# Attention scores of a float32 block: one float32 matmul per head in place of a product split into high and low parts

## The chip, the cores and the metric

The kernel runs on one core of one Trainium2 chip. The metric is the device time of one execution in microseconds (us), as the median of the runs; lower is better.

## The reference, cut to what matters

Eight sequences of 128 tokens with 512 features go through a layer norm, a cross-attention with 32 query heads and 8 key/value heads of 128 features, a gated residual, a second layer norm and a gated feed-forward layer. All of it is float32.

```python
q = (query @ Wq).reshape(nb, q_len, H, D).transpose(0, 2, 1, 3)
k = (key @ Wk).reshape(nb, q_len, KVH, D).transpose(0, 2, 1, 3)
...
q = q * cos + _rotate_half(q) * sin
k = k * cos + _rotate_half(k) * sin
...
scores = jnp.einsum('bhqd,bhkd->bhqk', q, k) / jnp.sqrt(jnp.float32(D))
scores = jnp.where(mask == 0, jnp.float32(-1000000000.0), scores)
attn = jax.nn.softmax(scores, axis=-1)
```

The mask holds a 1 where a position is masked out of the context and 0 elsewhere, one mask per sequence.

## The kernel before

TensorE multiplies in the reduced type float32r. To keep float32 accuracy each float32 operand is split: ScalarE (ACT) writes a rounded high part, GpSimd (POOL) or VectorE (DVE) writes the remainder as a low part, and TensorE (PE) adds three products: high by high, high by low, low by high. The helper `three` (L509 to L511) does this for the projections, the product with v, the output projection and the feed-forward layer.

Each engine runs an order of work written out by hand, held together by semaphores. A prologue (to about 115 us) transposes context and x, makes k and v for all heads, and stores both to scratch memory in HBM. Then come 64 attention steps, numbered n: a step is one sequence and one group of four query heads that share a key/value head. `pair(gg, c)` handles two steps, k = 0 and 1. In a pair PE makes two blocks of new queries (`q_block`, 12 matmuls of 512 columns each), scores, the transpose of the probabilities, the product with v (`pv`) and the output projection of an earlier pair. The feed-forward layer follows from about 584 us.

What the change touches, step by step:

- Rotation of queries and keys: DVE multiplies by cosine and sine (`rot_cos`, `rot_sin`), POOL adds the two (`add_q`, `add_k`) and so writes `q32` and `k32` in float32.
- Keys: `k_hi_copy` (ACT) and `k_lo_split` (POOL) write the high and low part side by side into `ks_parts`; SP's queue stores both to scratch (`store_k`) and later loads them into `k_parts` (`load_k`).
- Queries: `q_hi_copy` (ACT, L843) and `q_lo_split` (POOL, L1143) make `q_hi` and `q_lo` for each step.
- Scores (L632, L633): for each of four heads one matmul with q_hi over 256 columns (key high and low parts, side by side) and one with q_lo over 128 columns (key high part) that is added to the first half. The four heads fill two banks of PSUM, so a step's scores wait until the mask step of the step before has read them (`dve_mask >= n`).
- Mask and maximum: `mask_first` (DVE, L1432) adds the mask to the second half of the scores and writes `prob`; `mask_rest` (DVE, L1441, four custom instructions) adds the first half and takes the row minimum (the scores are negated). ACT's exponentials (L913) follow, then the reciprocal on DVE (L1451), then POOL's normalisation (`norm`, L1185), then PE's transposes (L515), which are float32 matmuls in transpose mode with an identity.

Of the kernel before, what the change touches and what calls it, by code (L numbers as in the profile page):

```python
# [76 lines left out]
def build(nc, x, ctx, pos, mask, g_x, g_f, Wq, Wk, Wv, Wo, w12, b12, w3, b3, out):  # L77
    table = nc.inline_tensor(rope_table(), "rope_table")
    table = table.ap() if hasattr(table, "ap") else table
    k_dram = nc.dram_tensor("k_scratch", [UNITS * 128, HB * 2 * S], F32, kind="Internal").ap()  # L80
# [16 lines left out]
    with es:  # L97
# [9 lines left out]
        q_hi, q_lo = place("q_hi", [128, 2, GH, S], F32R), place("q_lo", [128, 2, GH, S], F32R)  # L107
        k_parts = place("k_parts", [128, 2, HB, 2 * S], F32R)
# [26 lines left out]
        wk_hi = place("wk_hi", [128, 2, KT * 128], F32R, at["q_hi"])  # L135
        wk_lo = place("wk_lo", [128, 2, KT * 128], F32R, at["q_lo"])
        ks_parts = place("ks_parts", [128, 2, HB, 2 * S], F32R, at["o_hi"])
# [26 lines left out]
        s_parts = s_banks[:, :].rearrange("p (h two k) -> p h two k", h=GH, two=2)  # L164
# [24 lines left out]
        act_khi, pool_klo = sems("act_khi", "pool_klo")  # L189
        pe_v, act_vhi, dve_vlo = sems("pe_v", "act_vhi", "dve_vlo")  # L190
        act_qhi, pool_qlo = sems("act_qhi", "pool_qlo")
        pe_score, dve_masked, dve_mask = sems("pe_score", "dve_masked", "dve_mask")
# [164 lines left out]
        def _(sp):  # L357
# [25 lines left out]
            def store_k(kk):  # L383
                group, half = K_ORDER[kk]
                u = 2 * group + half
                sp.wait_ge(act_khi, kk + 1)
                sp.wait_ge(pool_klo, kk + 1)
                sp.dma_start(k_dram[u * 128:(u + 1) * 128, :], f32(ks_parts[:, kk % 2].rearrange("p b k -> p (b k)"))).then_inc(k_stored[kk % 2], 16)
# [12 lines left out]
            def load_k(half, group):  # L401
                sp.dma_start(f32(k_parts[:, half].rearrange("p b k -> p (b k)")),
                             k_dram[bass.ds(group * 256 + half * 128, 128), :]).then_inc(k_loaded[half], 16)
# [68 lines left out]
            def ffn_load(t):  # L472

                dst, s, _ = ffn_raw(t)
                if t < RAW:
                    sp.wait_ge(act_whi, CHUNKS - RAW + t + 1)
                    sp.wait_ge(pool_wlo, pool_split(CHUNKS - RAW + t))
                elif t == RAW:

                    sp.wait_ge(act_qhi, 4 * (UNITS - 1))  # L480
                    sp.wait_ge(pool_qlo, 4 * (UNITS - 1))
                for i in range(4):
                    sp.dma_start(dst[32 * i:32 * i + 32, :].rearrange("b (j f) -> b j f", j=4), ffn_src(t, i)).then_inc(s, 16)
# [14 lines left out]
            sp.wait_ge(pool_klo, UNITS)  # L498
# [8 lines left out]
        def _(pe):  # L507
# [114 lines left out]
            def scores(gg, c, k):  # L622
                n = n_of(gg, c, k)
                half, b = (c // 2) % 2, 2 * (c % 2) + k
                pe.wait_ge(act_qhi, n + 1)
                pe.wait_ge(pool_qlo, n + 1)
                if k == 0:
                    pe.wait_ge(k_loaded[half], 16 * (2 * gg + c // 4 + 1))
                if not (isinstance(n, int) and n < 1):
                    pe.wait_ge(dve_mask, n)  # L630
                for h in range(GH):
                    nc.tensor.matmul(s_banks[:, 256 * h:256 * (h + 1)], q_hi[:, k, h, :], k_parts[:, half, b, :], start=True, stop=False)  # L632
                    mm = nc.tensor.matmul(s_banks[:, 256 * h:256 * h + 128], q_lo[:, k, h, :], k_parts[:, half, b, 0:128], start=False, stop=True)  # L633
                mm.then_inc(pe_score, 1)
# [204 lines left out]
        def _(act):  # L839
# [54 lines left out]
            def q_hi_copy(gg, c, k):  # L894

                n = n_of(gg, c, k)
                b = 2 * (c % 2) + k
                if isinstance(n, int) and n < 2:
                    act.wait_ge(pool_rope, ROT_ORDER.index(("Q", 3)) + 1)
                else:  # L900
                    act.wait_ge(pool_rope, KBLOCKS + 16 * gg + 4 * (c // 2) + 4)
                if isinstance(n, int) and n < 2:

                    act.wait_ge(pe_kq, ROT_ORDER.index(("K", 6 + n, 1)) + 1)
                else:
                    act.wait_ge(pe_score, n - 1)
                hi(q_hi[:, k], q32[:, (c // 2) % 2, :, b * S:(b + 1) * S], act_qhi)

# [15 lines left out]
            def o_hi_copy(gg, c, k):  # L924
                n = n_of(gg, c, k)
                act.wait_ge(pe_pv, n + 1)
                if isinstance(n, int) and n < 2:

                    act.wait_ge(k_stored[0], 16 * KBLOCKS // 2)
                    act.wait_ge(k_stored[1], 16 * KBLOCKS // 2)  # L930
                else:
                    act.wait_ge(pe_out, n - 1)
                hi(o_hi[:, k], k4(pv_bank[:, :]), act_ohi)
# [8 lines left out]
            kk = vi = 0  # L942
            for i, blk in enumerate(STAGE):
# [5 lines left out]
                if i == 34:  # L949
                    q_hi_copy(0, 0, 0)  # L950
                if i == 35:
                    q_hi_copy(0, 0, 1)
                if i == 36:
                    exps(0, 0, 0)
                if i in (2, 3) or i > 3 and STAGE[i - 1][0] == "K":
                    k_hi_copy(kk)
                    kk += 1
# [13 lines left out]
            def first_pair():  # L971
# [3 lines left out]
                q_hi_copy(0, 1, 0)  # L975
                exps(0, 0, 1)
                q_hi_copy(0, 1, 1)
# [6 lines left out]
            def pair(gg, c):  # L984
# [6 lines left out]
                q_hi_copy(gg, c + 1, 0)  # L991
                o_hi_copy(gg, c, 0)
                pT_hi_copy(gg, c, 1)
                q_hi_copy(gg, c + 1, 1)
# [42 lines left out]
            q_hi_copy(3, 3, 0)  # L1037
# [4 lines left out]
            q_hi_copy(3, 3, 1)  # L1042
# [4 lines left out]
            q_hi_copy(3, 4, 0)  # L1047
# [3 lines left out]
            q_hi_copy(3, 4, 1)  # L1051
# [3 lines left out]
            q_hi_copy(3, 5, 0)  # L1055
            o_hi_copy(3, 3, 0)
            q_hi_copy(3, 5, 1)
# [8 lines left out]
            q_hi_copy(3, 6, 0)  # L1066
# [3 lines left out]
            q_hi_copy(3, 6, 1)  # L1070
            pT_hi_copy(3, 5, 0)
            o_hi_copy(3, 4, 1)
            q_hi_copy(3, 7, 0)
# [4 lines left out]
            q_hi_copy(3, 7, 1)  # L1078
# [52 lines left out]
        def _(pool):  # L1131
# [22 lines left out]
            def add_k(r, kk):  # L1154
                pool.wait_ge(dve_rot, r + 1)
                if kk >= 2:
                    pool.wait_ge(act_khi, kk - 1)
                    pool.wait_ge(pool_klo, kk - 1)
                nc.gpsimd.tensor_tensor(k32[:, kk % 2], t_cos[:, r % 2, :], t_sin[:, r % 2, :], ALU.add).then_inc(pool_rope, 1)

            def k_lo_split(kk):
                pool.wait_ge(act_khi, kk + 1)
                minus(ks_parts[:, kk % 2, :, S:2 * S], k4(k32[:, kk % 2]), f32(ks_parts[:, kk % 2, :, 0:S]), pool_klo)

            def add_q(gg, e, r=None):
# [6 lines left out]
                else:  # L1172

                    pool.wait_ge(act_qhi, 16 * gg + 4 * (e // 4) - 4)
                    pool.wait_ge(pool_qlo, 16 * gg + 4 * (e // 4) - 4)
                nc.gpsimd.tensor_tensor(q32[:, (e // 4) % 2, e % 4, :], t_cos[:, ts, :], t_sin[:, ts, :], ALU.add).then_inc(pool_rope, 1)  # L1176

            def q_lo_split(gg, c, k):
                b = 2 * (c % 2) + k
                pool.wait_ge(act_qhi, n_of(gg, c, k) + 1)  # L1180
                minus(q_lo[:, k], q32[:, (c // 2) % 2, :, b * S:(b + 1) * S], f32(q_hi[:, k]), pool_qlo)
# [12 lines left out]
            for i, blk in enumerate(STAGE):  # L1194
                if i == 34:
                    q_lo_split(0, 0, 0)
                if i == 36:
                    q_lo_split(0, 0, 1)
                    norm(0, 0, 0)
                if i and STAGE[i - 1][0] == "K":  # L1200
                    k_lo_split(kk)
                    kk += 1
                if blk[0] == "K":
                    add_k(r, kk)
                    r += 1
# [7 lines left out]
            def first_pair():  # L1213
                chunks = pair_chunks(0, 0)
                q_lo_split(0, 1, 0)
# [3 lines left out]
                q_lo_split(0, 1, 1)  # L1219
# [5 lines left out]
            def pair(gg, c):  # L1225
# [7 lines left out]
                q_lo_split(gg, c + 1, 0)  # L1233
                q_lo_split(gg, c + 1, 1)
# [15 lines left out]
            q_lo_split(3, 3, 0)  # L1250
# [4 lines left out]
            q_lo_split(3, 3, 1)  # L1255
# [4 lines left out]
            q_lo_split(3, 4, 0)  # L1260
            q_lo_split(3, 4, 1)
# [3 lines left out]
            q_lo_split(3, 5, 0)  # L1265
            add_q(3, 12)
            q_lo_split(3, 5, 1)
# [6 lines left out]
            q_lo_split(3, 6, 0)  # L1274
            q_lo_split(3, 6, 1)
# [4 lines left out]
            q_lo_split(3, 7, 0)  # L1280
            norm(3, 6, 1)
            q_lo_split(3, 7, 1)
# [12 lines left out]
        def _(dve):  # L1295
# [127 lines left out]
            def mask_first(gg, c, k):  # L1423

                n = n_of(gg, c, k)
                dve.wait_ge(pe_score, n + 1)
                if not (isinstance(n, int) and n < 2):
                    dve.wait_ge(pe_pT, n - 1)
                b = (2 * c + k) % B
# [5 lines left out]
            def mask_rest(gg, c, k):  # L1435

                n = n_of(gg, c, k)
                dve.wait_ge(dve_masked, n + 1)
# [6 lines left out]
            def mask_scores(gg, c, k):  # L1445
                mask_first(gg, c, k)
                mask_rest(gg, c, k)
# [39 lines left out]
            def pair(gg, c):  # L1487
# [4 lines left out]
                mask_first(gg, c, 1)  # L1492
                recip(gg, c, 0)
                mask_rest(gg, c, 1)
# [235 lines left out]
```

## Time and profile before

| | |
|---|---|
| median of 3 runs | 665.45 us (664.97 to 665.58) |
| span of the profiled execution, first to last instruction | 662.9 us |
| PE busy | 654.6 us (99% of the span), granted clock 1.000 |
| DVE, ACT, POOL busy | 490.2, 314.1, 385.5 us |
| DMA | 66.32 MB moved |

The profile gives the span of its execution and no separate device time for it; the median of the runs is 2.55 us above that span. Matmul records overlap: one begins while the one before still drains, so the time that a matmul occupies the engine is read from the distance between starts, not from its duration.

### The profile page before, as it was taken

To read this page: it belongs to the slowest core of one execution; us is meant where nothing else is said; L and a number is where in the kernel's file an instruction comes from. 1 tells how busy PE (TensorE), PEld (TensorE's weight loads), DVE (VectorE), ACT (ScalarE), POOL (GpSimd) and SP (SyncE) were. 2 spreads that over 40 slices of the span, in tenths; PEclk is the share of its full clock that TensorE was granted. 3 is DMA by queue.
4 is the path that set the end of the run, shared out by engine and by line. 5 is a ranking of instruction groups with operands and counts; after the bars stand their busy time and mean duration, and the time that the engine had idled before them with its cause. 6 is when DMAs were issued, how large, how long until landed. Compare 5 with 4: busy or idle time off the path is not lost.

```text
span 662.9 us, 11265 instructions
## 1 busy us (share of the span) xinstructions
PE 654.6 (99%) x3309; PEld 550.3 (83%) x3309; DVE 490.2 (74%) x1235; ACT 314.1 (47%) x891; POOL 385.5 (58%) x323
## 2 busy tenths in 40 slices
PE   8999999999999999999999999999999999989998
PEld 7888888788888888888888888888888888878886
DVE  3987665887777777777777777777777888986432
ACT  4335613545445445544554554554455566545210
POOL 6457767875566666666556666666655776402100
PEclk9999999999999999999999999999999999999999
DMA  9996983422212131312222121212122205000002
GB/s 302 321 325 210 306 303 105 143 62 99 91 39 97 44 99 34 95 32 96 62 80 95 34 98 45 95 32 95 63 76 75 58 10 151 0 1 1 0 33 95
DMA packets 67452, 66.32 MB, mean 100 GB/s; under 512 B 6608, under 2 KB 50640, under 8 KB 67408
## 3 DMA queue, kind: packets, MB, share of 16 engines
q1 hardware_dynamic: 65984, 64.77, 30.7%
q0 software_dynamic: 384, 1.05, 0.4%
q8 instruction: 17, 0.28, 0.2%
q14 instruction: 27, 0.22, 0.1%
q10 hardware_dynamic: 1040, 0.00, 0.1%
HBM read 46.93 MB, written 18.87 MB: 99 GB/s over the span
## 4 chain that ended last, share of the span: by engine, by line
PE 94%; DVE 2%; DMA 1%; issue 1%; POOL 0%; ACT 0%; DVEq 0%
PE f_bank L509 12%; PE f_bank L511 12%; PE f_bank L510 12%; PE o_bank L509 10%; PE o_bank L511 10%; PE o_bank L510 10%; PE s_banks L632 6%; PE t_bank L515 4%; PE pv_bank L509 3%; PE pv_bank L511 3%; PE pv_bank L510 3%; PE s_banks L633 2%; PE t_bank L511 1%; PE t_bank L509 1%; PE s_banks L511 1%; PE s_banks L510 1%
## 5 line engine op out<-in xcount | busy, mean ns | idle before, releaser
L1185 POOL TENSOR_TENSOR prob<-prob,small 128x512 f32<-128x512 f32 x64 | 66.6, 1040 | 124.9 <-DVE small L1451 124.9
L913 ACT ACTIVATE prob<-prob,small 128x128 f32<-128x128 f32 x256 | 99.8, 391 | 77.7 <-DVE small L1441 72.2
L509 PE MATMUL o_bank<-wo_hi,o_hi 128*128 128x512 f32 x248 | 102.1, 412 | 0.0
L1143 POOL TENSOR_TENSOR q_lo<-q,q_hi 128x512 fp32r<-128x512 f32 x64 | 82.7, 1292 | 32.8 <-ACT q_hi L843 32.8
L509 PE MATMUL f_bank<-xT_hi,wq_hi 128*128 128x512 f32 x256 | 101.6, 397 | 0.0
L843 ACT ACTIVATE o_hi<-pv_bank 128x512 fp32r<-128x512 f32 x64 | 38.3, 599 | 131.4 <-PE pv_bank L511 130.9
L511 PE MATMUL f_bank<-xT_hi,wq_lo 128*128 128x512 f32 x256 | 99.9, 390 | 0.0
L510 PE MATMUL f_bank<-xT_lo,wq_hi 128*128 128x512 f32 x256 | 99.8, 390 | 0.0
L511 PE MATMUL o_bank<-wo_hi,o_lo 128*128 128x512 f32 x248 | 97.4, 393 | 0.0
L510 PE MATMUL o_bank<-wo_lo,o_hi 128*128 128x512 f32 x248 | 96.9, 391 | 0.0
L1353 DVE TENSOR_TENSOR t_sin<-f_bank,rope 64x512 f32<-64x512 f32 x128 | 88.1, 689 | 2.8
L1176 POOL TENSOR_TENSOR q<-t_cos,t_sin 128x512 f32<-128x512 f32 x64 | 82.7, 1293 | 4.3 <-DVE t_sin L1353 4.2
L1441 DVE CUSTOM_DVE_ANT_0 prob<-s_banks,prob 128x128 f32<-128x128 f32 x256 | 59.1, 287 | 10.3 <-DVE prob L1432 7.7
L1353 DVE TENSOR_TENSOR t_cos<-f_bank,rope 128x512 f32<-128x512 f32 x64 | 43.9, 686 | 29.5 <-PE f_bank L511 29.4
L632 PE MATMUL s_banks<-k_parts,q_hi 128*128 128x256 f32 x256 | 62.8, 323 | 0.4 <-issue 0.2
L1465 DVE SCALAR_TENSOR_TENSOR resid<-o_bank,small,resid 128x512 f32<-128x512 f32 x62 | 46.4, 748 | 17.4 <-PE o_bank L511 16.2
L633 PE MATMUL s_banks<-k_parts,q_lo 128*128 128x128 f32 x256 | 56.9, 222 | 0.0
L511 PEld LDWEIGHTS f_bank<-xT_hi,wq_lo 128*128 128x128 f32 x256 | 48.1, 188 | 10.2
L509 PEld LDWEIGHTS f_bank<-xT_hi,wq_hi 128*128 128x128 f32 x256 | 48.1, 188 | 9.5 <-issue 0.4
L510 PEld LDWEIGHTS f_bank<-xT_lo,wq_hi 128*128 128x128 f32 x256 | 48.2, 188 | 9.1
L511 PEld LDWEIGHTS o_bank<-wo_hi,o_lo 128*128 128x128 f32 x248 | 46.6, 188 | 10.6
L1306 DVE TENSOR_TENSOR o_lo<-pv_bank,o_hi 128x512 fp32r<-128x512 f32 x64 | 44.0, 687 | 15.3 <-ACT o_hi L843 15.3
(170 smaller groups left out, 1469.5 us busy)
## 6 DMA issues: line engine op xcount, KB each, us to landing
k_scratch<-ks_parts SPq DMA_DIRECT2D x16, 512.0 KB, 3.1
raw<-in_L_xattn_Wq_dram SPq DMA_DIRECT2D x32, 256.0 KB, 2.8
raw<-in_L_xattn_Wo_dram SPq DMA_DIRECT2D x32, 256.0 KB, 2.6
k_parts<-k_scratch SPq DMA_DIRECT2D x16, 512.0 KB, 3.6
v_scratch<-vs_hi SPq DMA_DIRECT2D x16, 256.0 KB, 3.9
v_scratch<-vs_lo SPq DMA_DIRECT2D x16, 256.0 KB, 4.3
v_hi<-v_scratch SPq DMA_DIRECT2D x16, 256.0 KB, 3.9
v_lo<-v_scratch SPq DMA_DIRECT2D x16, 256.0 KB, 4.3
```

The costliest lines, as they stand in the source:

```text
L509: nc.tensor.matmul(dst, st[0], mv_[0], start=start, stop=False)
L510: nc.tensor.matmul(dst, st[0], mv_[1], start=False, stop=False)
L511: return nc.tensor.matmul(dst, st[1], mv_[0], start=False, stop=stop)
L632: nc.tensor.matmul(s_banks[:, 256 * h:256 * (h + 1)], q_hi[:, k, h, :], k_parts[:, half, b, :], start=True, stop=False)
L633: mm = nc.tensor.matmul(s_banks[:, 256 * h:256 * h + 128], q_lo[:, k, h, :], k_parts[:, half, b, 0:128], start=False, stop=True)
L913: e = nc.scalar.activation(prob[:, k, h, :], prob[:, k, h, :], ACT.Exp, bias=nmin[k][:, h:h + 1], scale=-1.0, accum_out=psum_row[k][:, h:h ...
L1143: nc.gpsimd.tensor_tensor(dst, a, b_, ALU.subtract).then_inc(s, 1)
L1176: nc.gpsimd.tensor_tensor(q32[:, (e // 4) % 2, e % 4, :], t_cos[:, ts, :], t_sin[:, ts, :], ALU.add).then_inc(pool_rope, 1)
L1185: nc.gpsimd.tensor_tensor(prob[:, k], prob[:, k], rrow[k].unsqueeze(2).to_broadcast([128, GH, S]), ALU.mult).then_inc(pool_norm, 1)
L1353: return nc.vector.tensor_tensor(dst, a, b_, ALU.mult)
L1441: op = nc.vector.tensor_tensor_reduce(prob[:, k, h, :], s_parts[:, h, 0, :], prob[:, k, h, :], 1.0, HUGE, ALU.add, ALU.min, nmin[k][:, h:h ...
L1465: nc.vector.scalar_tensor_tensor(out=resid[:, b, :], in0=bank_of_out(gg, c, k)[:, :], scalar=tg_x, in1=resid[:, b, :], op0=ALU.mult, op1=A ...
```

## The change

The scores become one float32 matmul per head of 128 columns, stationary `q32`, moving `k_ring` (the keys in float32). The split parts of q and k go, with the ACT and POOL instructions that make them; the scratch for k and the ring that it is loaded into are half as large. Each step's scores take one PSUM bank, and steps use the two banks in turn, so scores of step n wait for the mask of step n - 2 only. The mask is an operand of the four custom instructions; `mask_first` goes. Some waits change their source: the store of k waits for POOL's add, `add_k` waits for the store two blocks back to have landed, `add_q` waits for scores in place of the copies, scores wait for POOL's add, and the load of the last feed-forward weights waits for scores. The buffers `wk_hi` and `wk_lo` get space of their own.

```diff
-            def k_hi_copy(kk):
-                act.wait_ge(pool_rope, ROT_ORDER.index(("K",) + K_ORDER[kk]) + 1)
-                if kk >= 2:
-                    act.wait_ge(k_stored[kk % 2], 16 * (kk // 2))
-                hi(ks_parts[:, kk % 2, :, 0:S], k4(k32[:, kk % 2]), act_khi)
...
-                hi(q_hi[:, k], q32[:, (c // 2) % 2, :, b * S:(b + 1) * S], act_qhi)
...
-            def k_lo_split(kk):
-                pool.wait_ge(act_khi, kk + 1)
-                minus(ks_parts[:, kk % 2, :, S:2 * S], k4(k32[:, kk % 2]), f32(ks_parts[:, kk % 2, :, 0:S]), pool_klo)
...
-            def q_lo_split(gg, c, k):
-                b = 2 * (c % 2) + k
-                pool.wait_ge(act_qhi, n_of(gg, c, k) + 1)
-                minus(q_lo[:, k], q32[:, (c // 2) % 2, :, b * S:(b + 1) * S], f32(q_hi[:, k]), pool_qlo)
...
             def scores(gg, c, k):
                 n = n_of(gg, c, k)
                 half, b = (c // 2) % 2, 2 * (c % 2) + k
-                pe.wait_ge(act_qhi, n + 1)
-                pe.wait_ge(pool_qlo, n + 1)
                 if k == 0:
+                    if isinstance(n, int) and n == 0:
+                        pe.wait_ge(pool_rope, ROT_ORDER.index(("Q", 3)) + 1)
+                    else:
+                        pe.wait_ge(pool_rope, KBLOCKS + 16 * gg + 4 * (c // 2) + 4)
                     pe.wait_ge(k_loaded[half], 16 * (2 * gg + c // 4 + 1))
-                if not (isinstance(n, int) and n < 1):
-                    pe.wait_ge(dve_mask, n)
+                if not (isinstance(n, int) and n < 2):
+                    pe.wait_ge(dve_mask, n - 1)
                 for h in range(GH):
-                    nc.tensor.matmul(s_banks[:, 256 * h:256 * (h + 1)], q_hi[:, k, h, :], k_parts[:, half, b, :], start=True, stop=False)
-                    mm = nc.tensor.matmul(s_banks[:, 256 * h:256 * h + 128], q_lo[:, k, h, :], k_parts[:, half, b, 0:128], start=False, stop=True)
+                    mm = nc.tensor.matmul(s_bank[k][:, 128 * h:128 * (h + 1)], q32[:, (c // 2) % 2, h, b * S:(b + 1) * S], k_ring[:, half, b, :],
+                                          start=True, stop=True)
                 mm.then_inc(pe_score, 1)
...
             def add_k(r, kk):
                 pool.wait_ge(dve_rot, r + 1)
                 if kk >= 2:
-                    pool.wait_ge(act_khi, kk - 1)
-                    pool.wait_ge(pool_klo, kk - 1)
+                    pool.wait_ge(k_stored[kk % 2], 16 * (kk // 2))
...
-                nc.vector.tensor_tensor(prob[:, k], s_parts[:, :, 1, :], mfill[:, b, :].unsqueeze(1).to_broadcast([128, GH, S]),
-                                        ALU.add).then_inc(dve_masked, 1)
...
                 for h in range(GH):
-                    op = nc.vector.tensor_tensor_reduce(prob[:, k, h, :], s_parts[:, h, 0, :], prob[:, k, h, :], 1.0, HUGE,
+                    op = nc.vector.tensor_tensor_reduce(prob[:, k, h, :], s_bank[k][:, 128 * h:128 * (h + 1)], mfill[:, b, :], 1.0, HUGE,
                                                         ALU.add, ALU.min, nmin[k][:, h:h + 1])
```

## Rows read from the trace of the kernel before

**Rows 1.** The page: busy us, share of the span, instructions of each engine.

```profile
PE 654.6 (99%) x3309; PEld 550.3 (83%) x3309; DVE 490.2 (74%) x1235; ACT 314.1 (47%) x891; POOL 385.5 (58%) x323
```

**Rows 2.** The chain that ended last: shares of the span by engine.

```profile
PE 94%; DVE 2%; DMA 1%; issue 1%; POOL 0%; ACT 0%; DVEq 0%
```

**Rows 3.** Stretches: window, then busy us (count) of PE, PEld, DVE, ACT, POOL; clock.

```profile
300.00:400.00 100.00, 99.86 (x517) 84.30 (x516) 76.22 (x210) 50.20 (x164) 62.88 (x53) 1.00 0.25 78
```

**Rows 4.** Waits of PE: total us, times, longest us.

```profile
PE s_banks L515 <- ACT xnorm L1009: 1.9, 1, 1.9
...
PE s_banks L632 <- DVE small L1441: 0.2, 1, 0.2
```

**Rows 5.** Timeline of PE around one step's scores: start us, duration us, instruction.

```profile
301.36 0.28 PE L632 MATMUL s_banks<-k_parts,q_hi 128*128 128x256 f32 x1
301.47 0.22 PE L633 MATMUL s_banks<-k_parts,q_lo 128*128 128x128 f32 x1
...
302.23 0.45 PE L509 MATMUL f_bank<-xT_hi,wq_hi 128*128 128x512 f32 x1
302.51 0.40 PE L510 MATMUL f_bank<-xT_lo,wq_hi 128*128 128x512 f32 x1
302.75 0.39 PE L511 MATMUL f_bank<-xT_hi,wq_lo 128*128 128x512 f32 x1
...
304.79 0.39 PE L511 MATMUL f_bank<-xT_hi,wq_lo 128*128 128x512 f32 x1
305.02 0.60 PE L515 MATMUL t_bank<-ident,prob 128*128 128x128 f32 x4
305.37 0.48 PE L509 MATMUL o_bank<-wo_hi,o_hi 128*128 128x512 f32 x1
305.69 0.39 PE L510 MATMUL o_bank<-wo_lo,o_hi 128*128 128x512 f32 x1
```

**Rows 6.** Timeline of PE's weight loads for the same scores.

```profile
301.36 0.19 PEld L633 LDWEIGHTS s_banks<-k_parts,q_lo 128*128 128x128 f32 x1
...
302.05 0.19 PEld L633 LDWEIGHTS s_banks<-k_parts,q_lo 128*128 128x128 f32 x1
```

**Rows 7.** PE's groups by shape: busy us, mean ns of one.

```profile
L633 PE MATMUL s_banks<-k_parts,q_lo 128*128 128x128 f32 x256 | 56.9, 222 | 0.0
L515 PE MATMUL t_bank<-ident,prob 128*128 128x128 f32 x256 | 38.5, 272 | 0.2
```

**Rows 8.** Groups that the change removes, and the custom instruction beside them.

```profile
L1143 POOL TENSOR_TENSOR q_lo<-q,q_hi 128x512 fp32r<-128x512 f32 x64 | 82.7, 1292 | 32.8 <-ACT q_hi L843 32.8
L1143 POOL TENSOR_TENSOR ks_parts<-k,ks_parts 128x512 fp32r<-128x512 f32 x16 | 20.8, 1299 | 12.6 <-ACT ks_parts L843 12.6
L843 ACT ACTIVATE q_hi<-q 128x512 fp32r<-128x512 f32 x64 | 40.1, 626 | 9.6 <-POOL q L1176 8.3 <-PE f_bank L511 1.4
L843 ACT ACTIVATE ks_parts<-k 128x512 fp32r<-128x512 f32 x16 | 10.1, 633 | 25.8 <-POOL k L1159 25.8
L1432 DVE TENSOR_TENSOR prob<-s_banks,mfill 128x512 f32<-128x512 f32 x64 | 44.2, 691 | 6.5 <-PE s_banks L633 5.3 <-PE t_bank L515 0.7
```

**Rows 9.** Timeline of DVE, ACT and PE at the end of attention.

```profile
571.41 0.69 DVE L1432 TENSOR_TENSOR prob<-s_banks,mfill 128x512 f32<-128x512 f32 x1 [0.23 <-PE t_bank L515]
...
575.22 0.60 ACT L843 ACTIVATE pT_hi<-t_bank 128x512 fp32r<-128x512 f32 x1 [0.30 <-PE t_bank L515]
...
576.01 0.68 DVE L1306 TENSOR_TENSOR pT_lo<-t_bank,pT_hi 128x512 fp32r<-128x512 f32 x1
...
584.34 0.66 PE L515 MATMUL s_banks<-ident,xnorm 128*128 128x128 f32 x4 [1.86 <-ACT xnorm L1009]
```

**Rows 10.** DMA issues: count, KB each, median us from issue to landing.

```profile
k_scratch<-ks_parts SPq DMA_DIRECT2D x16, 512.0 KB, 3.1
...
k_parts<-k_scratch SPq DMA_DIRECT2D x16, 512.0 KB, 3.6
```

**Rows 11.** Waits of SP's queue: total us, times, longest us.

```profile
SPq L387 <- POOL ks_parts L1143: 54.2, 16, 10.6
```

More of the change, by code:

```diff
@@ L106, in build @@
         q32 = place("q32", [128, 2, GH, HT], F32)
-        q_hi, q_lo = place("q_hi", [128, 2, GH, S], F32R), place("q_lo", [128, 2, GH, S], F32R)
-        k_parts = place("k_parts", [128, 2, HB, 2 * S], F32R)
+        wk_hi, wk_lo = place("wk_hi", [128, 2, KT * 128], F32R), place("wk_lo", [128, 2, KT * 128], F32R)
+        k_ring = place("k_ring", [128, 2, HB, S], F32)
         v_hi, v_lo = place("v_hi", [128, 2, HB, D], F32R), place("v_lo", [128, 2, HB, D], F32R)
@@ L134, in build @@
         w3_all = place("w3_all", [128, KT, E], F32, at["wq_lo"])
-        wk_hi = place("wk_hi", [128, 2, KT * 128], F32R, at["q_hi"])
-        wk_lo = place("wk_lo", [128, 2, KT * 128], F32R, at["q_lo"])
-        ks_parts = place("ks_parts", [128, 2, HB, 2 * S], F32R, at["o_hi"])
         ffn_raw2 = place("ffn_raw2", [128, 4, 512], F32, at["q32"])
@@ L163, in build @@
         o_bank = [bank("o_bank0"), bank("o_bank1")]
-        s_parts = s_banks[:, :].rearrange("p (h two k) -> p h two k", h=GH, two=2)
+        s_bank = [s_banks[:, 0:512], s_banks[:, 512:1024]]
         up_bank = [f_bank[0][:, :], f_bank[1][:, :], s_banks[:, 0:512], s_banks[:, 512:1024]]
@@ L385, in store_k @@
                 u = 2 * group + half
-                sp.wait_ge(act_khi, kk + 1)
-                sp.wait_ge(pool_klo, kk + 1)
-                sp.dma_start(k_dram[u * 128:(u + 1) * 128, :], f32(ks_parts[:, kk % 2].rearrange("p b k -> p (b k)"))).then_inc(k_stored[kk % 2], 16)
+                sp.wait_ge(pool_rope, ROT_ORDER.index(("K", group, half)) + 1)
+                sp.dma_start(k_dram[u * 128:(u + 1) * 128, :], k32[:, kk % 2]).then_inc(k_stored[kk % 2], 16)
             v_rows = v_dram.rearrange("(h g t p) c -> h g t p c", h=2, g=KVH, t=2)
@@ L892, in x_norms @@
                     normalise(xnorm[:, b % 4, :], b)
-            def q_hi_copy(gg, c, k):
-                n = n_of(gg, c, k)
-                b = 2 * (c % 2) + k
[L898 to L906, printed above, removed]
-                hi(q_hi[:, k], q32[:, (c // 2) % 2, :, b * S:(b + 1) * S], act_qhi)
             def exps(gg, c, k):
@@ L926, in o_hi_copy @@
                 act.wait_ge(pe_pv, n + 1)
[L927 to L931, printed above, removed]
+                if not (isinstance(n, int) and n < 2):
                     act.wait_ge(pe_out, n - 1)
@@ L941, in _ @@
                 first_chunk(s)
-            kk = vi = 0
+            vi = 0
             for i, blk in enumerate(STAGE):
@@ L1194, in _ @@
             for i, blk in enumerate(STAGE):
-                if i == 34:
-                    q_lo_split(0, 0, 0)
                 if i == 36:
-                    q_lo_split(0, 0, 1)
                     norm(0, 0, 0)
-                if i and STAGE[i - 1][0] == "K":
-                    k_lo_split(kk)
-                    kk += 1
                 if blk[0] == "K":
                     add_k(r, kk)
+                    kk += 1
                     r += 1
@@ L1421, in _, with mask_scores @@
                     nc.vector.tensor_scalar(mfill[:, :, :], mask_raw[:, :, :], 0.0, MASKED, ALU.is_equal, ALU.mult).then_inc(dve_small, 1)
-            def mask_first(gg, c, k):
+            def mask_scores(gg, c, k):
                 n = n_of(gg, c, k)
+                b = (2 * c + k) % B
                 dve.wait_ge(pe_score, n + 1)
```

61 lines of the change are left out of this document (6 added, 55 removed).

## The prediction

> **What bounds the kernel now.** I read the busy times first, then the chain that ended last, then PE's waits, and only then single stretches. PE is busy for 654.6 of 662.9 us, no other engine for more than 74% [rows 1], and 94% of the chain is PE itself [rows 2]. In a stretch of steady attention PE is busy for 99.86 of 100 us at a granted clock of 1.00, the 2.4 GHz level, while DVE has 24, POOL 37 and ACT 50 us to spare [rows 3]. PE is idle for 8.3 us in all; its largest wait is 1.9 us for the second layer norm, and for the mask step it waits 0.2 us, once [rows 4]. So the reader is to see one thing: work taken from DVE, ACT or POOL is worth nothing by itself. The change is worth what it does to PE's own instructions, and a little at the waits.
>
> **What a step's scores cost PE today.** Starts count, not durations. Matmuls of 512 columns follow each other at (304.79 - 302.75) / 9 = 0.227 us [rows 5], 0.057 us for each 128 columns. The scores begin at 301.36; the projection after them begins at 302.23 and its second matmul at 302.51 [rows 5]. That first projection matmul takes 0.28 and not 0.227, because its weights could not be loaded ahead in time. So the scores displace 302.51 - 301.36 - 0.227 = 0.923 us. The columns explain less: 4 heads of 384 columns are 4 x 0.170 = 0.68 us. The loads explain it: eight, at (302.05 - 301.36) / 6 = 0.115 us each [rows 6], make 0.92 us. Scores today are bound by their weight loads. 64 steps cost 59 us.
>
> **What the float32 matmul costs: the open term.** Before has no float32 matmul outside transpose mode. Its bounds come from these rows.
>
> - Below: the transposes are float32, 128x128 against 128x128. Four of them displace 305.69 - 305.02 - 0.227 = 0.443 us, 0.111 us each [rows 5], about twice the 0.057 us of 128 float32r columns. The durations agree: 272 ns against 222 ns for 128 columns [rows 7], 50 ns more for an equal shape. If a head costs no more than one transpose, a step falls from 0.923 to 0.443, 0.48 less; 64 of them are 31 us.
> - Above: a float32 product written as four products of high and low parts, each with its own load at today's 0.115 us, is 0.46 a head and 1.84 a step: 0.917 x 64 = 59 us more.
> - Between: in a transpose one operand is an identity, so only the other needs its full width. Here both need it, which doubles the pass: 2 x 0.111 = 0.222 a head, 0.887 a step. Counted the other way: today's split streams three products, 384 columns; a full product adds low by low, 512 columns, 0.227 a head and 0.907 a step if two loads of 0.115 hide under it, which they just do.
>
> I take the middle of these two, 0.897 a step: the row for a float32 pass and the row for 512 columns agree within 2%, while the ends differ by a factor of four. That is 0.026 less than 0.923, times 64, 1.7 us less. Steps ahead of `pv` are bound by the same eight loads, so I give them the same price.
>
> The Trainium skill speaks against this middle at one place. TensorE: Matmul & The Clock Gate, section Terms, says that transpose mode makes a float32 matmul four times faster. By that rule a head would cost 4 x 0.111 = 0.444 us, as an estimate, and the sum would be 54 us more in place of 1.7 less; no run here shows a float32 matmul without that mode.
>
> **The wait between steps.** The scores of step n wait today for the mask of step n - 1, because all four heads fill both banks; afterwards for n - 2. That 0.2 us [rows 4] is the gain. The new waits on `pool_rope` replace waits on instructions that themselves waited for it, and the query blocks are ready a pair earlier, so nothing new is late there. `add_q` now waits for scores instead of copies before it overwrites `q32`. Queued behind it on POOL are chunk splits and normalisations, which PE needs. But the sine product that `add_q` also needs stands behind the mask of those very scores in DVE's order, so the new wait has always ended: nothing.
>
> **Work removed off the path.** DVE loses 64 x 691 ns = 44 us, ACT 64 x 626 + 16 x 633 ns = 50 us, POOL 64 x 1292 + 16 x 1299 ns = 103 us [rows 8]. PE hides all of it today; were PE not there, DVE would still be the fullest. The mask as an operand of the custom instructions changes one input from `prob` to `mfill`, both float32 in SBUF, so I leave their price alone.
>
> One place has no cover: the end of attention, where PE idles 1.86 us for the layer norm behind a row of DVE work [rows 9]. The mask add at 571.41 stands in that row and costs 0.69 plus about 0.2 until the next instruction. But later in the row DVE takes pT_lo at 576.01, and that needs ACT's pT_hi, which ends at 575.82. DVE cannot move ahead of it by more than 0.19, so of 0.9 us about 0.15 arrives; what is late next is PE's transpose.
>
> **Keys.** Stores and loads halve from 512 KB [rows 10]. The prologue is PE's, so this buys nothing. `add_k` now waits for a store to land, with SP's queue ahead of it; behind it on POOL stand weight splits that PE needs. A store lands 3.1 us after issue, and SP has waited 54.2 us in total for POOL's key split [rows 11], so SP is early rather than late. Store and reuse lie two key blocks apart, in most of the prologue with two value blocks of 12 matmuls between them, 4 x 12 x 0.227 = 11 us. Nothing; uncovered, each late store would cost PE up to its 3 us.
>
> **Sum.** 1.7 + 0.2 + 0.15 = 2.05 us off a span of 662.9: 660.85. The median of the runs is 665.45, 2.55 us above the span; I carry that over and predict 663.4 us.
>
> **Rivals.**
>
> 1. Loads stay the bound. If a float32 head still needs two loads and each takes its 0.115 plus a few ns as today, a step is 0.92 to 0.95 us. For: loads bind today [rows 6]. Against: the transposes run at 0.111 with loads in their stream [rows 5]. Between 0 and +1.7 us on PE, less 0.35 at the waits: 665 to 666.5, no change that can be told.
> 2. Loads are not hidden at all. After a short pass the next load shows as 0.05 us today (0.28 against 0.227) [rows 5]. If each head pays that, 0.05 x 4 x 64 = 13 us come on top: 676 us. It decides once more than 0.02 us a head is exposed (0.02 x 256 = 5 us).
> 3. Four full passes, the other side at its plainest: 0.444 to 0.46 a head, so 1.77 to 1.84 a step, 54 to 59 us more on an engine that has no room to hide it: 719 to 724 us. For: four products are what two full-width operands hold, and today's split leaves one out to save time. Against: the 0.111 of a transpose is already twice a float32r pass, so four times that would count the width twice. It decides as soon as a head takes more than 0.231 us, today's price. The skill's rule on transpose mode, above, is this rival.
> 4. One pass, as cheap as a transpose: 665.45 - 31 = 634 us. For: same type and shape [rows 7]. Against: the row carries an identity.
>
> **How the numbers follow.** Forecast 0.43, with its own range of 661.5 to 664.1; rival 1 0.16; rival 2 0.13; rival 3 0.22; rival 4 0.06. A measurement of this kernel tells about 0.2% (1.3 us) from no change. The forecast and rival 4 are faster: 0.49. Rival 1 is the same, 0.14 of it within the bound and 0.02 beyond. Rivals 2 and 3 are slower: 0.37 with that. Leaving out rival 3 would leave more than 2 in 10 outside, so the range reaches over it: 661 to 722. Only rival 4 and the edges lie outside.
>
> **What would show it.** In the profile after, the distance from the first score matmul to the second matmul behind the scores, less 0.227, is the step's price: 0.89 right, 0.92 rival 1, 1.1 rival 2, 1.8 rival 3, 0.44 rival 4. The number of load and matmul records per head tells the passes. q_lo, q_hi and L1432 must be gone from POOL, ACT and DVE, with the span unmoved by it. PE's wait on the mask at 0.2 us must be gone, and the wait before the layer norm's transposes should stay near 1.7 us. Wrong would be a wait of POOL on the key store, or PE waiting for `pool_rope`.

## The result, and the profile after

| | before | after |
|---|---|---|
| median, us (4 runs each) | 665.21 (664.97 to 665.58) | 660.7 (660.45 to 661.0) |
| ratio of the medians | | 0.9932, 95% interval 0.9918 to 0.9946 |
| span of the profiled execution, us | 662.9 | 659.0 |

The change made the kernel faster by 4.5 us; 663.4 was predicted, and 660.7 lies just under the low edge, 661. The direction and the price of the float32 matmul came out as forecast. The gain at the waits was several times the forecast, and the price of the scores before was read too low.

The page of the profile after, busy time and chain, answers to [rows 1] and [rows 2]:

```profile
PE 651.8 (99%) x3309; PEld 549.5 (83%) x3309; DVE 448.1 (68%) x1171; ACT 271.4 (41%) x811; POOL 285.8 (43%) x243
...
PE 96%; DMA 1%; DVE 1%; POOL 0%; issue 0%; ACT 0%
```

DVE lost 42 us, ACT 43 and POOL 100, about what [rows 8] promised, and PE 2.8. PE's count of 3309 is the same as before: 512 pairs of load and matmul for the scores then, 512 now. The groups of the scores' line say so, with mean ns of one at the end:

```profile
L626 PE MATMUL s_banks<-k_ring,q 128*128 128x128 f32 x512 | 67.3, 274 | 0.0
...
L626 PEld LDWEIGHTS s_banks<-k_ring,q 128*128 128x128 f32 x512 | 66.7, 191 | 4.7
```

There are 256 heads in 64 steps, so one float32 matmul of the program is two loads and two matmuls on the engine. Each lasts 274 ns, beside 272 for a transpose [rows 7]. The stretch in steady attention and PE's waits, as in [rows 3] and [rows 4]:

```profile
300.00:400.00 100.00, 100.00 (x517) 84.41 (x517) 69.29 (x199) 42.96 (x144) 48.51 (x41) 1.00 0.19 58
```

```profile
PE s_banks L507 <- ACT xnorm L967: 1.7, 1, 1.7
PE pv_bank L583 <- POOL ident L1082: 1.5, 1, 1.5
PE pv_bank L501 <- issue: 0.6, 1, 0.6
```

The wait for the mask is gone, no wait on `pool_rope` has come, and the layer norm's has gone from 1.86 to 1.69 us. The timeline of PE around a step, as in [rows 5]:

```profile
298.95 1.05 PE L626 MATMUL s_banks<-k_ring,q 128*128 128x128 f32 x8
299.76 0.48 PE L501 MATMUL f_bank<-xT_hi,wq_hi 128*128 128x512 f32 x1
300.07 0.40 PE L502 MATMUL f_bank<-xT_lo,wq_hi 128*128 128x512 f32 x1
```

The step's price is 300.07 - 298.95 - 0.227 = 0.893 us; 0.897 was forecast. Starts are printed to 0.01 us, so a price read from two of them can be off by as much. By the starts in ns that the trace holds, the 52 steps between 137 and 531 us cost 0.930 us each in before (0.928 to 0.931) and 0.895 in after (0.894 to 0.895).

**Where the 3.9 us of span came from.** PE's matmuls outside the scores are the same in both traces and in the same order, so I subtracted start from start. The difference grows in stages (after minus before, worked out from the two timelines of PE):

| stretch of before, us | gained, us | predicted, us |
|---|---|---|
| start, up to 43 us (first loads) | 0.14 | 0 |
| first four score steps, 114 to 137 | 1.22 | some 0.3 (0.2 for the mask wait, 4 x 0.026) |
| 52 steps, 137 to 531, without the next row | 1.84 | 1.4 (52 x 0.026) |
| two turns of the loop over pairs, at 260 and 381 | 0.25 + 0.34 | 0 |
| last eight steps, 531 to 580 | -0.13 | 0.2 |
| layer norm, from 580 | 0.21 | 0.15 |

The start is no effect of the change: profiles of the variants below differ there by up to 0.47 us, and it is taken off their differences.

**The first score step.** Here is the trace of before on POOL, on PE's weight loads and on PE, at the first scores:

```profile
113.34 1.29 POOL L1143 TENSOR_TENSOR q_lo<-q,q_hi 128x512 fp32r<-128x512 f32 x1 [0.74 <-ACT q_hi L843]
...
114.70 0.19 PEld L632 LDWEIGHTS s_banks<-k_parts,q_hi 128*128 128x128 f32 x1 [0.59 <-issue]
...
114.14 0.39 PE L511 MATMUL f_bank<-cT_hi,wk_lo 128*128 128x512 f32 x1
114.73 0.36 PE L632 MATMUL s_banks<-k_parts,q_hi 128*128 128x256 f32 x1 [0.20 <-issue]
```

and PE of after at the same place:

```profile
114.01 0.39 PE L503 MATMUL f_bank<-cT_hi,wk_lo 128*128 128x512 f32 x1
114.23 1.05 PE L626 MATMUL s_banks<-k_ring,q 128*128 128x128 f32 x8
```

POOL's q_lo ends at 114.63, the load follows at 114.70; without q_lo the scores follow the matmul ahead by 0.22 us, not 0.59. The releaser is given as "issue", with 0.20 on PE because the last matmul's record still drains, and with 0.59 on the weight loads. A reader who goes by PE's waits alone sees a third of it.

**The turns of the loop.** Here are ACT's wait row, its timeline at 256 us and the instruction queue's row (packets, MB, share) of the trace of before:

```profile
ACT prob L913 <- issue: 5.3, 2, 2.7
...
256.49 0.40 ACT L913 ACTIVATE prob<-prob,small 128x128 f32<-128x128 f32 x1 [2.61 <-issue]
...
q14 instruction: 27, 0.22, 0.1%
```

In after, ACT has no such row, and the queue moves fewer packets:

```profile
q14 instruction: 16, 0.13, 0.1%
```

ACT stands still for 2.6 us at each of two turns, by the profile without another engine to wait for, and PE's transposes come late by 0.25 and 0.34 us.

### The profile page after: what moved, and what is told of

Read it like the earlier page. It is cut to its first block, busy times and chain, and to the rows that moved or that the text cites. A ratio compares the mean times of both kernels' runs of the same rounds, so it can differ in the third digit from the quotient of the medians.

```text
span 659.0 us, 10792 instructions
## 1 busy us (share of the span) xinstructions
PE 651.8 (99%) x3309; PEld 549.5 (83%) x3309; DVE 448.1 (68%) x1171; ACT 271.4 (41%) x811; POOL 285.8 (43%) x243
## 4 chain that ended last, share of the span: by engine, by line
PE 96%; DMA 1%; DVE 1%; POOL 0%; issue 0%; ACT 0%
PE f_bank L503 12%; PE f_bank L501 12%; PE f_bank L502 12%; PE o_bank L501 10%; PE o_bank L503 10%; PE o_bank L502 10%; PE s_banks L626 9%; PE t_bank L507 4%; PE pv_bank L501 3%; PE pv_bank L503 3%; PE pv_bank L502 3%; PE t_bank L501 1%; PE t_bank L503 1%; PE s_banks L503 1%; PE s_banks L501 1%; PE s_banks L502 1%
## 5 line engine op out<-in xcount | busy, mean ns | idle before, releaser
L1352 DVE CUSTOM_DVE_ANT_0 prob<-s_banks,mfill 128x128 f32<-128x128 f32 x256 | 59.2, 287 | 20.5 <-PE s_banks L626 14.3
L626 PEld LDWEIGHTS s_banks<-k_ring,q 128*128 128x128 f32 x512 | 66.7, 191 | 4.7
L626 PE MATMUL s_banks<-k_ring,q 128*128 128x128 f32 x512 | 67.3, 274 | 0.0
L1224 DVE TENSOR_TENSOR pT_lo<-t_bank,pT_hi 128x512 fp32r<-128x512 f32 x64 | 43.9, 686 | 23.6 <-ACT pT_hi L837 23.5
L1091 POOL TENSOR_TENSOR wq_lo<-raw,wq_hi 128x512 fp32r<-128x512 f32 x35 | 45.0, 1290 | 29.8 <-ACT wq_hi L837 29.8
L1091 POOL TENSOR_TENSOR wo_lo<-raw,wo_hi 128x512 fp32r<-128x512 f32 x32 | 41.2, 1292 | 35.8 <-ACT wo_hi L837 35.8
```

Source lines behind the costliest of these rows:

```text
L626: mm = nc.tensor.matmul(s_bank[k][:, 128 * h:128 * (h + 1)], q32[:, (c // 2) % 2, h, b * S:(b + 1) * S], k_ring[:, half, b, :], start=True ...
L1091: nc.gpsimd.tensor_tensor(dst, a, b_, ALU.subtract).then_inc(s, 1)
L1224: nc.vector.tensor_tensor(dst, src, f32(hi_part), ALU.subtract).then_inc(s, 1)
L1352: op = nc.vector.tensor_tensor_reduce(prob[:, k, h, :], s_bank[k][:, 128 * h:128 * (h + 1)], mfill[:, b, :], 1.0, HUGE, ALU.add, ALU.min, ...
```

## The experiments

Theory after the result: the matmul gives 1.8 us over the steps, and the rest comes from waits of the first steps and at the turns, each ended by another part of the change. Rival: everything comes from the matmul, through a shorter step that moves the waits as well. Edits are against the kernel after, unless said otherwise.

**Parts put back, one at a time.** First the copies of q: q_hi and q_lo are made again, and the scores wait for both but read q32.

```diff
             def scores(gg, c, k):
+                pe.wait_ge(act_qhi, n + 1)
+                pe.wait_ge(pool_qlo, n + 1)
...
+                q_hi_copy(gg, c + 1, 0)
...
+                q_lo_split(gg, c + 1, 0)
```

> The changed kernel with q_hi (ACT) and q_lo (POOL) made again for every step, read by nobody, and the scores waiting for them as before. Theory of parts: the first step of attention waits again for POOL's q_lo (0.5 us), and ACT's loop, 16 instructions longer per turn, stands still for 2.6 us at its two turns again, of which 0.25 to 0.35 us each reach PE: 1.0 to 1.2 us more than the changed kernel, about 661.8. Rival (freed ACT and POOL speed PE up all along): 2 us more or above, spread evenly over the 64 steps.

661.29 us, ratio to before 0.9945 [0.9933, 0.9958], span 659.6. PE is later by 0.44 us at the first score step and by nothing more in the steps behind it. The weight loads' wait is back, this row of the waits of PE's loads:

```profile
PEld s_banks L630 <- issue: 0.6, 1, 0.6
```

The standstill of ACT, which I expected back as well, isn't. So the first step's wait hung on the copies, the standstill on something else.

Then the wait between steps:

```diff
-                if not (isinstance(n, int) and n < 2):
-                    pe.wait_ge(dve_mask, n - 1)
+                if not (isinstance(n, int) and n < 1):
+                    pe.wait_ge(dve_mask, n)
```

> The changed kernel with one number changed: the scores of step n wait for the mask of step n - 1 instead of n - 2, as if there were one bank. Theory of parts: only the first steps feel it, 0 to 0.4 us more, near 661.0. Rival (a bank per batch is what brings the gain): 1.5 us more or above.

661.14 us, 0.9942 [0.9929, 0.9955], span 659.3. Nothing in the first four steps; about 0.1 us at one place of each of the loop's three rounds (138, 258 and 378 us), 0.29 in all.

Then the mask add, as an instruction of its own on DVE, whose result the custom instructions overwrite:

```diff
+                nc.vector.tensor_tensor(prob[:, k], s_bank[k].rearrange("p (h k) -> p h k", h=GH), mfill[:, b, :].unsqueeze(1).to_broadcast([128, GH, S]),
+                                        ALU.add).then_inc(dve_masked, 1)
```

> The changed kernel with the mask add of 691 ns put back on DVE ahead of the four custom instructions, in the order of the kernel before; its output is written over. Theory of parts: DVE has room in steady attention, so 0 to 0.4 us more, at the first steps and at the layer norm behind attention (0.15 us): near 661. Rival (DVE's 44 us were what held PE): 1.5 us more or above.

661.5 us (660.99 to 662.99), 0.9945 [0.9932, 0.9958]. PE is later by 0.27 us by 137 us and by 0.43 behind the wait for the layer norm at 580, which takes 0.14 of it. The profiled execution is the longest, 661.2 us of span, for a reason of its own. These are the windows of its end of attention (PE, PEld, DVE, ACT, POOL busy, granted clock), and the matmul that ended its wait for the layer norm:

```profile
580.00:582.00 2.00, 0.96 (x6) 0.90 (x7) 1.99 (x4) 1.79 (x3) 0.00 (x0) 1.00 0.00 0
582.00:584.00 2.00, 2.00 (x9) 1.69 (x8) 1.31 (x2) 2.00 (x5) 0.00 (x0) 0.59 0.00 0
584.00:586.00 2.00, 2.00 (x7) 1.58 (x6) 1.95 (x3) 0.70 (x2) 0.00 (x0) 0.56 0.00 0
586.00:590.00 4.00, 4.00 (x24) 3.37 (x23) 1.69 (x3) 2.31 (x3) 0.00 (x0) 1.00 0.01 4
...
581.04 0.66 PE L507 MATMUL s_banks<-ident,xnorm 128*128 128x128 f32 x4 [1.82 <-ACT xnorm L967]
```

After PE had idled 1.82 us, the granted clock fell to means of 0.59 and 0.56 in the next two windows, mostly the 1.2 GHz level, and stood at 1.00 (2.4 GHz) from 586 us on. PE was busy without a gap meanwhile. Before idled 1.86 us there and kept 1.00, so the length of the wait alone didn't decide it. Nor did the kernel: of 15 executions of before that were measured with the last variants, four had a mean granted clock of 0.997 over the span, as this one had, and took 666.6 to 667.9 us; the others took 664.9 to 665.8. What decided it is open.

All three together leave of the change the float32 matmul, the missing split of k and the bank for each step:

> The changed kernel with everything but the matmul put back: the query copies on ACT and POOL and the wait of the scores for them, the wait for the mask of step n - 1, and the mask add on DVE. Theory of parts (a step's scores cost PE 0.893 us instead of 0.93, and the rest of the gain is a handful of single waits that the removed work caused): 64 x 0.04 = 2.5 us below the kernel before, about 662.7 us, with the single waits back. Rival (the freed engines let PE run faster all along): nearly all of the gain is lost, 664.5 us or more. Rival (the matmul is worth nothing, waits are everything): 665.

662.6 us, 0.9965 [0.9952, 0.9978], span 660.8, step price 0.893. Later than after by 0.44 us at the first step, 1.14 by 137 us and 1.3 at 580. One at a time they gave 0.71 by 137 us; the other 0.43 came only with all three, I suppose because a longer mask step then meets scores that wait for it. So 1.1 of the 1.22 us in the first four steps are the waits of these three parts, and the matmul isn't their cause.

**The price of the float32 matmul.** Every score matmul twice:

```diff
-                for h in range(GH):
+                for h in [i // 2 for i in range(2 * GH)]:
```

> The changed kernel with each score matmul issued twice, with the same operands. Theory: PE is the bound and has no room, so the price of the second set is added whole. If float32 heads cost 0.222 us a piece: 64 x 4 x 0.222 = 57 us more, span near 716. Rival (part of the price is hidden or is paid at the edges of the set): 50 us more or less than that.

721.22 us (one run), span 719.4. PE's timeline around a step:

```profile
300.22 1.95 PE L626 MATMUL s_banks<-k_ring,q 128*128 128x128 f32 x16
301.92 0.48 PE L501 MATMUL pv_bank<-pT_hi,v_hi 128*128 128x512 f32 x1
302.24 0.40 PE L502 MATMUL pv_bank<-pT_lo,v_hi 128*128 128x512 f32 x1
```

302.24 - 300.22 - 0.227 = 1.793 us, and 1.788 by the starts in ns: the second set costs 0.893 beside 0.895 for the first, a price that repeats, 0.112 us for each pair of load and matmul. The span is 3 us longer than the 716 that I expected, because PE's loop, longer now, brought a standstill to PE itself at its two turns, with more packets in its queue (17 in before and after):

```profile
PE f_bank L501 <- issue: 3.5, 2, 2.0
...
q8 instruction: 37, 0.61, 0.4%
```

Which half of a pair binds, half as many columns tell:

```diff
-                    mm = nc.tensor.matmul(s_bank[k][:, 128 * h:128 * (h + 1)], q32[:, (c // 2) % 2, h, b * S:(b + 1) * S], k_ring[:, half, b, :],
+                    mm = nc.tensor.matmul(s_bank[k][:, 128 * h:128 * h + 64], q32[:, (c // 2) % 2, h, b * S:(b + 1) * S], k_ring[:, half, b, 0:64],
```

> The kernel after, with scores made for 64 of the 128 key positions only; half of the scores are left out. Loads stay as they are, two of 128 columns for each head. Theory: the float32 matmul is bound by its columns, 0.111 us for 128 in each of the two matmuls. Then the price of a step falls from 0.89 to between 0.45 and 0.6 us and the time to 634 to 642 us. Rival: the two loads of a head set the price, and the columns just fit beneath them. Then a step stays at 0.86 to 0.89 us and the time at 659 to 661 us.

662.48 us, 0.995 [0.9928, 0.9971], span 660.6. PE's timeline:

```profile
295.51 1.00 PE L626 MATMUL s_banks<-k_ring,q 128*128 128x64 f32 x8
296.31 0.48 PE L501 MATMUL pv_bank<-pT_hi,v_hi 128*128 128x512 f32 x1
296.63 0.39 PE L502 MATMUL pv_bank<-pT_lo,v_hi 128*128 128x512 f32 x1
```

296.63 - 295.51 - 0.227 = 0.893 us, as with all the columns. The columns aren't the bound; the loads, or something else that a pair pays whatever its width, are. By the starts in ns the step's price is 0.897, beside 0.895. The span is still 1.6 us longer than after's; that gathers in the matmuls of 512 columns between the scores, and I can't explain it.

And one float32r matmul a head, with q and k written in that type:

```diff
-        q32 = place("q32", [128, 2, GH, HT], F32)
+        q32 = place("q32", [128, 2, GH, HT], F32R)
...
-        k_ring = place("k_ring", [128, 2, HB, S], F32)
+        k_ring = place("k_ring", [128, 2, HB, S], F32R)
```

> The kernel after, with q and k rounded to float32r as they are written, and one float32r matmul for each head; the low parts of q and k are left out. Theory: a float32 matmul is two pairs of load and matmul, so one pair is left, and with 128 columns of float32r it is bound by the load: 4 x 0.115 = 0.46 us a step, 0.43 less than now, 27.5 us in all, 633 us. Rival 1: the columns set it, 4 x 0.057 = 0.23 us a step, 42 us in all, 618 us. Rival 2: the second pair of a float32 matmul hides under the first and costs nothing. Then the time hardly falls, 655 to 661 us.

632.59 us, 0.9496 [0.9467, 0.9525]. PE's timeline:

```profile
284.66 0.56 PE L626 MATMUL s_banks<-k_ring,q 128*128 128x128 f32 x4
285.05 0.45 PE L501 MATMUL pv_bank<-pT_hi,v_hi 128*128 128x512 f32 x1
285.34 0.40 PE L502 MATMUL pv_bank<-pT_lo,v_hi 128*128 128x512 f32 x1
```

Four pairs in place of eight, 285.34 - 284.66 - 0.227 = 0.453 us, and 0.450 by the starts in ns, 0.113 each. 64 x (0.895 - 0.450) = 28.5 us, beside 28.2 between the spans, 659.0 and 630.8. Four, eight and sixteen pairs cost 0.450, 0.895 and 1.788 us: with up to 128 columns the price counts pairs, and neither type nor columns.

**The standstill at the turns.** Counted over ACT's instructions, without the records that only wait, its loop over pairs stands at 115 to 344 in before and at 95 to 304 in after. First, copies of one column on ACT ahead of the loop, 40 and then 24 of them, so that its end stands at 344 again, or at 328:

```diff
+                if 8 <= i < 28:
+                    for j in range(2):
+                        nc.scalar.activation(small[64 * j:64 * j + 64, 92 + i:93 + i], ident[64 * j:64 * j + 64, 0:1], ACT.Copy)
```

> The changed kernel with 40 tiny copies put on ACT ahead of its loop over pairs, so that the loop ends at ACT instruction 344 of its program, as in the kernel before. Theory: ACT's standstill of 2.6 us at the two turns of its loop in the kernel before came from where the loop lies in its program (it ended at 344 there and at 304 in the changed kernel); it comes back, and PE loses 0 to 0.35 us at each turn: 0 to 0.7 us more than the changed kernel. Rival (it came from ACT's work on q inside the loop): no standstill.

> The same with 24 tiny copies, so that ACT's loop ends at instruction 328, where the loop of the kernel with the query copies put back ended without a standstill. Theory of position: no standstill at the loop's turns. If any added work ahead of the loop brings it, it shows here as well.

660.85 us (0.9933 [0.9914, 0.9952]) and 661.01 us (one run): no standstill, 16 packets in both. The end's place alone isn't it. Then q's copies again with 16 such copies, which puts the loop at 115 to 344 and at its old length:

> The variant with q's copies made again (661.3 us), and 16 copies of one column each on ACT in the prologue, so that ACT's loop over pairs stands at instruction 115 to 344 of ACT's program, as in the kernel before (99 to 328 without them). Theory: the standstill of ACT at the turns of its loop comes from the length and the place of the loop's code. Then it is back: ACT idle with issue for about 2.6 us twice, some 27 packets in the instruction queue of ACT in place of 16, PE late by 0.25 to 0.35 us at each of two turns, 661.8 to 662.0 us. Rival: it came from other work of the kernel before. Then no standstill, 16 packets, 661.3 us.

661.72 us, 0.9934 [0.9911, 0.9957], span 659.6 as without the 16: again no standstill. Place and length by this count aren't enough either. Last, the other way round, 20 such copies in the kernel before:

> The kernel before with 20 copies of one column each on ACT in the prologue, so that ACT's loop stands at instruction 135 to 364 in place of 115 to 344; its length, 229, stays. Theory: the place of the loop's code decides about the standstill. A loop that began at 135 had none, so it is gone: no issue of 2.6 us on ACT, 16 or 17 packets in its instruction queue in place of 27, and about 0.6 us less than before, 664.5 us. Rival: the length decides, 229 against 209 without a standstill. Then it stays, 665.1 us.

664.2 us, 0.9981 [0.9969, 0.9993]. ACT's first instruction behind the same turn, the one that started at 256.49 in before, and the queue's row:

```profile
254.60 0.40 ACT L913 ACTIVATE prob<-prob,small 128x128 f32<-128x128 f32 x1 [0.51 <-DVE small L1444]
...
q14 instruction: 17, 0.14, 0.1%
```

The standstill is gone with nothing removed from the kernel, and the packets with it: ACT waits 0.51 us for DVE and starts. With its start taken off, PE keeps its times of before up to the first turn, and is earlier by 0.30 us over that turn and by 0.34 over the second; the medians stand 1.1 us apart. So it is a matter of where the code lies. The rule that decides is open. The Trainium skill, Runtime: NRT & Kernel Launch, section Instruction fetch mechanics, says that most engines hold two blocks of 256 instructions and that a taken branch to a place outside them must wait for a fetch. The extra packets agree with a fetch. If the records that only wait count as instructions too, which is a guess, the loops stand at 171 to 452 (before), 191 to 472 (20 copies), 155 to 436 (q's copies and 16) and 171 to 416 (40 copies). Then a block that ends at some place from 181 to 191 would leave before's loop alone in three blocks. That fits all runs, but it was fitted to them and not tried on a new one.

**A version that beats both kernels.** At the end of attention after, POOL's three subtractions for the feed-forward weights run just when DVE takes its small steps of the layer norm. Timeline of POOL, DVE and PE:

```profile
574.00 3.79 POOL L1091 TENSOR_TENSOR w_lo<-w_all,w_hi 128x512 fp32r<-128x512 f32 x3
...
574.37 0.95 DVE L1238 TENSOR_SCALAR small<-small 128x4 f32<-128x4 f32 x1
575.36 1.22 DVE L1239 TENSOR_SCALAR small<-small 128x4 int32<-128x4 int32 x1
576.61 1.21 DVE L1244 SCALAR_TENSOR_TENSOR small<-small 128x4 f32<-128x4 f32 x1
577.85 0.16 DVE L1245 TENSOR_TENSOR small<-small 128x4 f32<-128x4 f32 x1
...
580.49 0.65 PE L507 MATMUL s_banks<-ident,xnorm 128*128 128x128 f32 x4 [1.69 <-ACT xnorm L967]
```

Three instructions on four columns take about 1 us each, the next, past POOL's end, 0.16. One line lets POOL start after them:

```diff
+            pool.wait_ge(dve_shift, 2)
             ffn_lo(4)
             ffn_lo(5)
```

> The changed kernel with one wait more: POOL holds its four low parts of the first feed-forward weights behind attention back until DVE has finished the statistics of the second layer norm (dve_shift >= 2). In the changed kernel three DVE instructions on 128x4 values take 0.95, 1.22 and 1.21 us there while POOL runs three subtractions of 1.26 us; their like take 0.16 us after them. Theory: POOL's subtractions hold those three up, so they drop to about 0.2 us, DVE's row ends 2.9 us sooner and PE's wait of 1.7 us for the layer norm goes: 1.5 to 1.7 us less than the changed kernel, near 659. Rival: the three are slow by themselves (first use of an operation); then POOL's order changes nothing, 660.7.

659.03 us (658.67 to 659.25), 0.9904 [0.9888, 0.992], span 657.4. The same rows:

```profile
574.71 0.16 DVE L1239 TENSOR_SCALAR small<-small 128x4 f32<-128x4 f32 x1
574.91 0.17 DVE L1240 TENSOR_SCALAR small<-small 128x4 int32<-128x4 int32 x1
575.11 0.16 DVE L1245 SCALAR_TENSOR_TENSOR small<-small 128x4 f32<-128x4 f32 x1
...
577.12 3.79 POOL L1091 TENSOR_TENSOR w_lo<-w_all,w_hi 128x512 fp32r<-128x512 f32 x3 [2.72 <-DVE small L1255]
...
579.00 0.60 PE L507 MATMUL s_banks<-ident,xnorm 128*128 128x128 f32 x4
```

0.95, 1.22 and 1.21 us become 0.16, 0.17 and 0.16, and PE's wait is gone. The three were slow because of POOL and not by themselves. This is the fastest version here that computes the scores with both operands in float32.

## Why the prediction was right and wrong

**The price of a step: right number, by luck.** 0.897 was forecast, 0.895 measured. I took the middle of two routes, and neither gives the mechanism. The doubling of the first is there: a head is two pairs of load and matmul, each at a transpose's price. But half the columns cost the same, so it is no pass that is paid by its columns, and the 512 columns of the second route don't set the price either. What a step pays is eight pairs of load and matmul, as before, and that is nearest to rival 1 (loads stay the bound), at 0.112 us a pair in place of the 0.115 and more that rival 1 took over from before. That it is the load that binds in a pair isn't shown apart from the rest of the pair. The transposes' 0.111 was a sound row, I suppose because they pay by the pair as well. Why the pairs of before took 0.116 (0.930 / 8) and these 0.112 isn't settled. Rivals 2 to 4 fall: a head takes 0.224 us, two transposes and not four, so by this trace the rule of the Trainium skill (TensorE: Matmul & The Clock Gate, section Terms) would double the price that was measured.

**The price of before: mis-sized.** I read 0.923 from two printed starts. By the starts in ns the same step is 0.931, and no step between 137 and 531 us is under 0.928: the 0.008 were rounding, and I multiplied them by 64. The difference to 0.895 is 0.035, and 0.035 a step arrived (1.84 / 52), where 0.026 was forecast. The last eight steps gained nothing: transposes follow six of them, and from the first score to the second transpose these take 0.993 to 0.998 us in before and 0.997 to 0.998 in after.

**The wait between steps: the step that failed.** "That 0.2 us [rows 4] is the gain", and "nothing new is late there". What was late already wasn't counted: 1.22 us came in the first four steps. The wait for q_lo at the first one, 0.44 us by the first experiment, stood in the views of before as "issue" on PE's weight loads. I took PE's largest named waiter and passed over the rows without a name. The mask wait of 0.2 us in PE's row was likewise only a part: at that step, the fourth, PE came 0.45 us earlier. With all three parts put back 1.14 of the 1.22 us were gone again.

**Work removed off the path: half right.** 185 us went from DVE, ACT and POOL, and steady attention gained nothing by it: with the work put back a step still costs 0.895. But "PE hides all of it today" left out ACT's two standstills, worth 0.59 us. They don't come from its work but from where its code lies, and the change moved that code.

**Layer norm: right.** 0.15 forecast, 0.21 measured (the mask add put back takes 0.14 of it), and 1.69 us of the wait stay. What holds DVE in that row was misread, though. Beside pT_lo it is POOL's subtractions, as the last experiment shows.

**Keys: right.** Here are the DMA groups of after, and the row of SP's queue that answers to [rows 11]:

```profile
k_scratch<-k SPq DMA_DIRECT2D x16, 256.0 KB, 2.2
k_ring<-k_scratch SPq DMA_DIRECT2D x16, 256.0 KB, 2.8
...
SPq L382 <- POOL k L1106: 40.3, 14, 9.3
```

Half the bytes land 0.9 and 0.8 us sooner than in [rows 10], SP still waits for POOL and not POOL for SP, and nothing of it reaches PE.

**The time around the span.** I carried over 2.55 us from before; after has 1.7 (660.7 - 659.0), and its profiled execution took 1.85 (660.85 - 659.0). In the later executions of before, too, the time is only 1.8 to 1.9 us above the span (664.87 and 663.0 in one of them), so the profile of before was of a shorter execution than its median. Of the 2.7 us between 663.4 and 660.7, 0.85 are this and 1.85 the span: 1.22 - 0.3 in the first steps, 0.59 at the turns, 0.14 at the start, and the rest from the steps, the last eight of which take 0.3 back.

## What to carry to other kernels

On an engine that is busy 99% of its span, price a repeated step by the mean of many of its instances, since one pair of printed starts is good to 0.01 us only and 64 steps make 0.6 us of that, and add up every idle row of it and of its weight loads, those put down to "issue" first: here they were worth as much as the change of the instruction. A matmul on up to 128 columns pays here for its pair of load and matmul, 0.112 us (0.116 a pair in the split before, with 128 and 256 columns in turn), so count pairs before columns. Where an edit lengthens or shortens a loop's program, look for standstills at its turns and at the packets of the instruction queues before crediting the work that was removed.

## What the runs showed of the hardware that wasn't expected

- A float32 matmul of 128 columns is two pairs of load and matmul, 0.224 us; with 64 columns it costs the same (0.897 beside 0.895 us for four heads), and one in float32r 0.113.
- An engine can stand still at the turn of its loop: ACT for 2.6 us with 27 packets in its instruction queue against 16 or 17, and PE, in the variant with doubled scores, for up to 2.0 us with 37 against 17.
- While POOL subtracts 128x512 elements, three DVE instructions on 128x4 take 0.95 to 1.22 us and not 0.16 to 0.17, and each ends 0.02 to 0.03 us after one of POOL's. The Trainium skill, Trainium Architecture — The Big Picture, section What this means for kernel authors, says that DVE and GpSimd share a pair of ports by an exclusive lock; the rows agree with a lock that holds until POOL's instruction ends.
- After a wait of 1.82 us the granted clock fell to 0.59 in one profiled execution; after one of 1.86 us in another kernel it stayed at 1.00, and the mean over the span differs between executions of one kernel (0.997 in four of 15 of before).
